# A two-layer attention and expert network on one core: three score banks in rotation, head pairs in halves of the partitions, a finer order of steps, and weights issued by GpSimd

## What is computed

```
x = x + xattn0(layernorm(x), ctx, ctx)     # 16 heads of 8, 512 keys, biases
x = x + ffn0(layernorm(x))                 # 8 experts 128-512-128, gelu, top 1 by a softmax gate
x = x + xattn1(layernorm(x), ctx)          # 16 query heads, 8 key heads, int8/ternary rounded
                                           # projections, a layernorm before the output projection
x = x + ffn1(layernorm(x))                 # shared expert + 15 experts 128-128-128, relu, top 3
scores = q @ k.T / sqrt(8); attn = softmax(scores); out = attn @ v      # per head
```

## Time and profile before

| | us |
|---|---|
| runs shown: 285.79, 287.11, 289.53; median | 287.11 |
| profiled execution, span from first to last instruction | 281.9 |
| median less span (start and end that the profile does not hold) | 5.2 |
| PE busy in the span | 235.6 |
| DVE busy | 177.7 |
| ACT busy | 145.3 |
| GpSimd busy | 54.4 |

### The profile page before, as it was taken

How to read it: one execution, slowest core, us unless ns; L and a number is a source line. 1 busy time by engine, 2 the same in 40 slices (tenths; PEclk the granted TensorE clock), 3 DMA queues, 4 the chain that set the end, 5 groups by cost and what they waited for, 6 DMA issues and landing times.

```text
span 281.9 us, 4880 instructions
## 1 busy us (share of the span) xinstructions
PE 235.6 (84%) x1685; PEld 152.1 (54%) x1700; DVE 177.7 (63%) x478; ACT 145.3 (52%) x336; POOL 54.4 (19%) x92
## 2 busy tenths in 40 slices
PE   2186345889999999999999999699699979889995
PEld 1035101344453545789988998343244424679985
DVE  5964797767656831421247137999577892589855
ACT  2026000657767686644435544366577678544542
POOL 8733982040402210100011300110000011021000
PEclk9999999799999999999999999959999999999999
DMA  6016327302270575800000110002100000000000
GB/s 158 0 60 226 150 72 162 110 4 80 74 205 22 149 190 137 215 5 2 1 0 0 58 56 2 1 0 58 56 4 0 3 0 0 3 0 0 21 1 20
DMA packets 20917, 16.26 MB, mean 58 GB/s; under 512 B 2085, under 2 KB 18989, under 8 KB 20797
## 3 DMA queue, kind: packets, MB, share of 16 engines
q1 hardware_dynamic: 20284, 15.76, 19.8%
q10 hardware_dynamic: 576, 0.13, 0.2%
q0 software_dynamic: 32, 0.07, 0.2%
HBM read 11.73 MB, written 4.19 MB: 56 GB/s over the span
## 4 chain that ended last, share of the span: by engine, by line
PE 65%; DVE 15%; ACT 7%; DMA 6%; issue 3%; SPq 2%; POOL 0%; DVEq 0%; ACTq 0%; another core or an unknown queue 0%
PE SB L1289 10%; PE OB L1226 8%; PE SA L1186 8%; DVE mx L906 7%; PE SB L1211 6%; PE OB L1302 5%; PE SB L1332 5%; PE SA L1302 5%; DMA Q<-nm 4%; PE SA L1342 4%; ACT prob L721 3%; DVE hn L871 3%; PE X L1154 2%; DVE qp L450 2%; PE X L1163 1%
## 5 line engine op out<-in xcount | busy, mean ns | idle before, releaser
L906 DVE TENSOR_REDUCE mx<-SA 128x1 bf16<-128x512 f32 x128 | 81.5, 686 | 20.0 <-PE SA L1186 15.9
L721 ACT ACTIVATE prob<-SB 128x512 f32<-128x512 f32 x128 | 69.4, 594 | 34.3 <-PE SB L1211 33.9
L1186 PE MATMUL SA<-K,Q 128*128 128x512 bf16 x113 | 41.5, 430 | 15.9 <-DVE mx L906 7.7
L1211 PE MATMUL SB<-Q,K 128*128 128x256 bf16 x256 | 41.6, 284 | 4.0 <-DMA Q<-nm 3.6
L782 ACT ACTIVATE prob<-SB,b1T 128x256 f32<-128x256 f32 x64 | 26.7, 471 | 28.5 <-PE SB L1289 28.4
L1226 PE MATMUL OB<-prob,V 128*32 128x256 f32 x512 | 39.7, 390 | 0.4 <-ACT oT L729 0.4
L1211 PEld LDWEIGHTS SB<-Q,K 128*128 128x128 bf16 x256 | 24.0, 101 | 24.9 <-ACT prob L721 6.8
L1289 PE MATMUL SB<-hT,w1s 128*128 128x256 f32 x128 | 33.3, 384 | 0.1
L1186 PEld LDWEIGHTS SA<-K,Q 128*128 128x128 bf16 x128 | 9.9, 102 | 35.6 <-DVE mx L906 23.9
L604 POOL TENSOR_SCALAR vareps<-mv 128x2 f32<-128x2 f32 x10 | 1.9, 192 | 137.2 <-DVE mv L850 137.2
L1289 PEld LDWEIGHTS SB<-hT,w1s 128*128 128x128 f32 x128 | 22.3, 190 | 3.6 <-ACT prob L782 0.7
(11 more groups left out here) (210 smaller groups left out, 282.4 us busy)
## 6 DMA issues: line engine op xcount, KB each, us to landing
w1s<-in_L_ffn_w_dram SPq DMA_DIRECT2D x8, 256.0 KB, 3.7
w2s<-in_L_ffn_w_dram SPq DMA_DIRECT2D x8, 256.0 KB, 4.4
K<-in_L_ffn_eW_dram SPq DMA_DIRECT2D x2, 960.0 KB, 6.5
K<-k_dram SPq DMA_DIRECT2D x8, 192.0 KB
Q<-q_dram SPq DMA_DIRECT2D x8, 192.0 KB
k_dram<-kp SPq DMA_DIRECT2D x2, 384.0 KB, 2.8
q_dram<-qp SPq DMA_DIRECT2D x4, 192.0 KB, 2.1
K<-k_dram SPq DMA_DIRECT2D x2, 384.0 KB
```

Source lines behind the costliest of these rows:

```text
L721: act.activation(prob[:, g % 2, i, 2 * u:2 * u + 2, :].rearrange("p k q -> p (k q)"), SB[u][:, :], ACT.Exp).then_inc(s_exp, 1)
L906: dve.tensor_reduce(mx[:, g % 2, r, i:i + 1], SA[SCORE_BANK[n]][:, :], AX, ALU.max).then_inc(s_sa_max, 1)
L1186: pe.matmul(SA[SCORE_BANK[u]][:, :], Q[n][:, b, s, r * P:(r + 1) * P], K[n][:, b, key_group(n, s), :], start=True, stop=True).then_inc(s_s ...
L1211: last = pe.matmul(SB[u][:, k * NQ:(k + 1) * NQ], K[n][:, b, key_group(n, s), kt * P:(kt + 1) * P], Q[n][:, b, s, :], start=True, stop=True)
```

## The change

One large rewrite of the order and of the layout of the stacks. In its parts:

- **Stack.** Row `8 * e + j` of the partitions now holds product `j` (0 to 5) of element `e`; `j` = 6 is the row of the maximum, `j` = 7 is zero. Head `2p` has partitions 0 to 63, head `2p + 1` has 64 to 127, so `Q` is half as large, and each score matmul reads 64 partitions (`rows`), the two heads of a pair alternating.
- **Write and read.** Each part is signalled, written once (one DMA each) as soon as it is made, and read back by six DMAs of 16 partitions each. ACT makes the first part straight from PSUM, DVE the rest. The queries of batch 0, layer 0 are read by ACT's queue.
- **Banks.** `X1` is now `SB[2]`: three `SB` banks rotate in attention, `X0` alone serves the small steps between the first and the last `exp` of a layer. The prologue uses idle `SA`, `SB`, `OB` banks.
- **Order.** Every `scores`, `values` and `max_rows` stands at a hand-written place; the lists are all new. The second batch's projections and `ctx_quant` come after the first `scores`. `values` waits for half a group's exponentials. `out_turn` and `bias0` are split or moved.
- **Who does what.** DVE zeroes `K[0]`, `Q[0]` (four memsets, now ahead of the first norm), GpSimd `K[1]`, `Q[1]`, `V` (smaller, 9 columns per head in place of 32). Some `max_rows`, `turn`, `vproj` copies move between ACT and DVE. GpSimd issues all bulk weights and small loads (`load`), and the row of ones of `K`.
- **Two DMAs** in place of one per `max_rows` (one per half).

```diff
-K_PART = (0, 1, 2, 0, 1, 0)
-SHIFT_ROW = 8 * len(K_PART)
-K_PARTS = ((2, 1), (1, 1))
+K_PART = (0, 0, 0, 1, 1, 2)
+SHIFT_ROW = 6
+STACK = 64
+K_PARTS = ((1, 1), (1, 1))
...
 IN_ATTENTION0 = {
...
+    (-2, 1): [('scores', 0, 3), ('scores', 1, 0)],
+    (-2, 2): [('zeros', 1, 1), ('max_rows', 0), ('values_ones', 1)],
+    (-2, 3): [('ctx_quant',)],
+    (-1, 0): [('w1_quant',), ('scores', 1, 1), ('qproj', 0, 1), ('vproj', 0, 1)],
+    (-1, 2): [('scores', 1, 2), ('scores', 1, 3)],
+    (-1, 3): [('kproj', 0, 1), ('ctxq_turn', 1), ('load_small', 0), ('ctxq_turn', 0), ('kstack', 0, 1),
+        ('scores', 2, 0)],
+    (0, 0): [('scores', 2, 1), ('max_rows', 1)],
...
+    (5, 2): [('out_turn', 0, 0, 0), ('kstack', 1, 1), ('scores', 7, 3), ('values', 4, 2)],
...
+    (7, 1): [('values', 6, 1), ('load_expert', 2), ('load_expert', 3)],
...
-        X = [stack.enter_context(nc.psum_tensor(f"X{n}", [P, 512], F32)) for n in range(2)]
-        YB = [OB, SA[2]]
+        X = [stack.enter_context(nc.psum_tensor("X0", [P, 512], F32)), SB[2]]
+        V0_BANK = [SA[2], OB]
+        YB = [SA[2], OB]
...
+        def read_stack(engine, dst, row_parts, dram, written, slots, done):
+            for part in range(3):
+                engine.wait_ge(written[part], 16)
+                for row in (j for j, p in enumerate(row_parts) if p == part):
+                    engine.dma_start(dst[row:P:8, slots].rearrange("e s c -> e (s c)"),
+                                     dram[part, :, slots].rearrange("e s c -> e (s c)")).then_inc(done, 16)
...
+                elif kind in LOADS and step not in ON_SYNC:
+                    load(pool, step)
...
+                    for a in range(2):
...
+                        rows = slice(64 * a, 64 * a + STACK)
+                        pe.matmul(SA[SCORE_BANK[u]][:, :], Q[n][rows, b, p, r * P:(r + 1) * P], K[n][rows, b, key_group(n, p), :],
                                   start=True, stop=True).then_inc(s_sa_full, 1)
...
+                    for a in range(2):
+                        m = 8 * gg + 2 * i + a
+                        if m >= 3:
+                            pe.wait_ge(s_exp, m - 2)
+                        rows = slice(64 * a, 64 * a + STACK)
                         for k in range(2):
                             kt = 2 * u + k
-                            last = pe.matmul(SB[u][:, k * NQ:(k + 1) * NQ],
-                                             K[n][:, b, key_group(n, s), kt * P:(kt + 1) * P], Q[n][:, b, s, :],
+                            last = pe.matmul(SB[m % 3][:, k * NQ:(k + 1) * NQ],
+                                             K[n][rows, b, key_group(n, p), kt * P:(kt + 1) * P], Q[n][rows, b, p, :],
                                              start=True, stop=True)
...
+                    if kt % 2 == 0:
+                        pe.wait_ge(s_exp, 8 * gg + 2 * kt + 4)
```

More of the change, by code:

```diff
@@ L78 @@
[L78 to L87, removed]
-IN_ATTENTION0 = {
[L89 to L110, removed]
@@ L111 @@
 }
 IN_EXPERTS00 = {
[L113 to L118, removed]
+    (-1, 1): [('out_turn', 0, 1, 0), ('out_turn', 0, 1, 1)],
+    (1, 0): [('att_turn', 0, 1)],
+    (1, 1): [('out_proj', 0, 1), ('stats', 'f0', 1)],
+    (3, 1): [('bias0', 0), ('norm', 'f0', 1)],
+    (6, 1): [('turn', 'f0', 1)],
+    (7, 0): [('red0', 1)],
@@ L119 @@
+    (7, 1): [('end0', 0)],
 }
 IN_EXPERTS01 = {
-    (-1, 0): [("end0", 0), ("stats", "q1", 0)],
-    (-1, 1): [("kstack", 1, 1), ("norm", "q1", 0), ("logits0", 1)],
-    (0, 0): [("quant", "q1", 0)],
-    (1, 0): [("bias0", 1), ("turn", "q1", 0)],
-    (1, 1): [("qproj", 1, 0)],
-    (4, 1): [("scores", 8, 0)],
-    (5, 0): [("scores", 8, 1)],
-    (5, 1): [("scores", 8, 2), ("qstack", 1, 0)],
-    (6, 0): [("scores", 8, 3)],
-    (6, 1): [("scores", 9, 0)],
+    (-1, 1): [('stats', 'q1', 0), ('logits0', 1)],
@@ L131 @@
+    (0, 1): [('norm', 'q1', 0)],
+    (1, 0): [('quant', 'q1', 0)],
+    (2, 0): [('turn', 'q1', 0)],
+    (2, 1): [('qproj', 1, 0)],
+    (5, 0): [('scores', 8, 0)],
+    (5, 1): [('scores', 8, 1), ('qstack', 1, 0)],
+    (6, 0): [('scores', 8, 2)],
+    (6, 1): [('scores', 8, 3)],
+    (7, 0): [('scores', 9, 0), ('scores', 9, 1)],
 }
 IN_ATTENTION1 = {
[L133 to L137 removed]
@@ L573, in _ @@
+                    for a in range(2):
+                        row = 64 * a + SHIFT_ROW
+                        sp.dma_start(Q[n][row:row + 1, b, 2 * g:2 * g + 2, :],
+                                     nm[2 * a:2 * a + 2, step[1] % 2, :]).then_inc(s_shift[step[1] % 2], 16)
+                elif kind in LOADS and step in ON_SYNC:
+                    load(sp, step)
                 elif kind == "store":
@@ L688, in _ @@
+                    parts_free(act, step)
+                    rows = P // (n + 1)
+                    dst, src = kp[0:rows, part_buffer(step), 0, :], xbank(step)[0:rows, :]
+                    if n == 0:
+                        act.wait_ge(in_bias0, 32)
+                        last = act.activation(dst, src, ACT.Identity, bias=bias3[:, 1:2])
+                    else:
+                        last = act.activation(dst, src, ACT.Copy)
+                    last.then_inc(s_kp[n][b], 1)
                 elif kind == "qproj":
@@ new lines, in _ @@
+                    u = part_buffer(step)
+                    if kind == "kproj":
+                        rows, bias, done = P // (n + 1), bias3[:, 1:2], s_kp[n][b]
+                        src, rest, parts = xbank(step)[0:rows, :], kr[0:rows, u, :], kp[0:rows, u, :, :]
+                    else:
+                        bias, done = bqs[:, :], s_qp[n][b]
+                        src, rest, parts = xbank(step)[:, 0:NQ], qr[:, u, :], qp[:, u, :, :]
+                    dve.wait_ge(done, 1)
+                    if n == 0:
+                        last = dve.scalar_tensor_tensor(rest, src, bias, parts[:, 0, :], ALU.add, ALU.subtract)
+                    else:
+                        last = dve.tensor_tensor(rest, src, parts[:, 0, :], ALU.subtract)
```

1017 lines of the change are left out of this document (598 added, 419 removed).

## The result

The changed kernel takes 275.66 us (median of 4 runs, 274.73 to 277.78), the kernel before 286.45 in the same session: a ratio of 0.9675, 95% interval 0.9587 to 0.9763. I forecast 262.5 us (248 to 277): the time lies inside the range, but the gain is 3.3% where I forecast 8.6%.

The account below looks back on a forecast made before the run. PE was taken to bound all but prologue and gap, DVE close behind in attention 1. Terms -5.8, -10, -1.3, 0, -6, -1.5 = -24.6 gave 257.3 us span, plus 5.2 to the median: 262.5 us, range 248 to 277.

Parts of the forecast that it names:

- The step: One attention step on PE: 1.55 us falls to 1.23 us, freeing 10 us of PE per layer.
- the bounds on the `scores` pair: Score matmuls in attention: nothing overlaps and a step keeps 1.55 us, or full overlap, `scores` part 0.33 instead of 0.54.
- Prologue: Start to first `exp`: first scores at 28 us against 34, first `exp` at 43.5 us against 49.3.
- +5.5: Prologue: DVE's four memsets, a reduce and the second stats stand before the norm, adding 5.5 us against 6.5 saved.
- Attention 0: First attention stage: 52 us against 62, from DVE's remaining scores steps, ACT's last `exp` steps, values and group 1's start.
- Experts and gap: Experts 0 65.4 us (-1), gap unchanged at 4 us, experts 1 37.4 us (-1.5).
- GpSimd's issues: Rival at the first `hidden0`: weight loads issued late while DVE and GpSimd hold each other up, 322 us; chance 0.03.
- Attention 1: Second attention stage: 55 us against 61, including +2 for batch 1's later queries.
- in part the slow clock at its start costs as now: Start of attention 1: the slow clock costs the same as before, 0.57 in 182 to 190 us.
- My 53: Attention 1 before the +2 for queries: 30.5 us and 9 us of DVE, 12.5 of `exp` steps, values 1.
- my marks of a wrong forecast: Steps of 1.5 us, stack waits over 2 us in attention, `hidden0` waiting for weights, or clock under 1 through much of attentions.
- PE stays the bound: Rival in both attentions: row halves do not overlap or switches eat the gain; 276.5 us, chance 0.20.

Follow-up runs that it names:

- the clearing run on all rows: Changed kernel with 128-row score matmuls, batch 0's layer-1 queries read for batch 1, SyncE's stack reads moved behind maxima rows, routed weights held for query reads: 276.80 us.
- the pair of cleared runs: Changed kernel without batch 1's layer-1 query wait, SyncE's stack reads moved, routed weights held: 276.80 us with 128-row score matmuls, 273.65 us in halves.

## Why the prediction was right and wrong

*The step.* Right. I took 1.23 us; it is 1.20. Of the bounds on the `scores` pair, overlap and no overlap, the lower came true, 0.30. By the Trainium skill, "TensorE: Matmul & The Clock Gate", Part 3, matmuls in different row groups run together, and the trace agrees; the drain at a change of tiling of its page "TensorEngine Tiling (Array Packing)", Key Properties, costs nothing beyond the 0.11 us that I had read from the trace. What I got wrong is who then bounds: where attention 0 runs steadily the chain still names PE at 1.20 a step and not DVE's reduces at 1.3, I take it because not every step has its two reduces. Over the whole of attention 0 PE is less than half of the chain; SyncE's stack reads (L510, 13%) and DMA landings stand beside it, and I had neither in the sum.

*Prologue.* 45.2 for 43.5. First reduce 29.9 us (28 forecast), `csq` from 36.99 to 42.94 (35.6 to 41.3), PE waiting for it with `exp 0` behind it, as described. The 1.7 us are within what the stack's landing with weights in flight costs: without them the first `exp` comes at 42.2. Of the memsets that I priced into +5.5, the 2.67 us that one run moved away are hidden.

*Attention 0.* 51.8 for 52, but partly by luck: other profiles of the same stage have 54.0 to 54.6. The mechanism holds in part: PE's busy time is 12.3 us less than before (58.43 to 46.09), but without the overlap the stage is 56.7 to 59.2 us, so the overlap gave 4 to 5 of the 10 us that I took for it, and the new order the rest.

*Experts and gap.* 67.1 for 65.4 and 39.5 for 37.4. The gains of 1 and 1.5 us that I gave to earlier norms and to halves among the experts did not come; PE is busy 65.29 us there, as before.

*GpSimd's issues.* Right. PE never waits for `w1s`, and no stall of several microseconds per issue shows.

*Attention 1.* Wrong: 64.8 for 55. Two terms of the sum failed. The step "from their projection to their use stand four `scores` steps, 5 us, and the way over DRAM takes some 8; +2" was mis-sized: the clearing run on all rows puts the whole of that way at 65.5 - 60.3 = 5.2 us, since the six reads also hold a row of maxima on SyncE and the routed weights are in flight beside the writes (2.9 us by itself, by the run in halves with all loads on SyncE). The larger one: "in part the slow clock at its start costs as now". It costs more. In halves PE's busy time fell from the 53.5 us before only to 52.5, though the work is less: 52.5 x 0.82 = 43.1 us at full clock, which is the 43 of my forecast. So the overlap was there, and the clock took 9.4 us of PE's time, against 53.5 x 0.06 = 3.2 before (estimates, since the clock is a mean over idle time too). With the way cleared it is 49.3 x 0.86 = 42.4 against 52.1 x 0.97 = 50.5 on all rows: 8 us less work, 2.8 us less busy time, 0.5 us less stage. How much the stage itself lost by the clock is shown only in that pair, 2.1 us ahead of the 17th exponential. The rest is no clock: behind it, at 1.00 in both, 5.1 us less of PE gave 2.5 us, since PE waits longer for others (in halves 3.9 us for maxima, 2.5 for exponentials, 1.8 for rows; 3.7, 1.8 and 0.8 on all rows). My 53 had the stage go by DVE's and ACT's work alone. The last of my marks of a wrong forecast, a clock under 1 through much of an attention, is what came; I had it as a mark and in no rival, so no time was worked out from it. Another, a wait of over 2 us for a stack inside an attention, came too, with 2.1 us.

*The rivals.* The time is within 1 us of the 276.5 that I gave to "PE stays the bound", and that is chance: its reason, halves that do not overlap or lose it all in switches, did not come, and its stages (60 and 61 us) are not those measured (51.8 and 64.8). My range holds the measured time only because I had drawn its upper end out to that rival.

By terms: prologue +1.7, attention 0 -0.2, experts 0 and gap +2.2, attention 1 +9.8 (about 3 the queries' way; the other 6.6 are the clock, of which PE's busy time allows at most some 6 and the pair of runs shows 2.1, and waits of PE that I had not counted, in shares that stay open), experts 1 +2.1: 15.6 of span. The median lay 2.8 us over the profiled span and not 5.2: -2.4, and 262.5 + 15.6 - 2.4 = 275.7.

What stays open: why the clock is low where it is. Shown is that of two orders alike in all but rows, the one on 64 rows without overlap stood at 0.70 and 0.58 and the one on 128 rows at 1.00 and 0.92, and that halves which overlap had 0.99 and 0.82. Whether it is the rows at work or the shorter busy stretches that overlap leaves in attention 1 isn't separated. A layout in halves that also keeps the clock up was not found, and no version beat the changed kernel by more than the measurement tells.

## What to carry to other kernels

An engine-time saving on PE is worth its size only at the clock that is granted afterwards: multiply PE's busy time by the granted clock of the stage, before and after, and if the product fell and the busy time did not, look for the clock and not for a new wait. And cut the stage where the clock changes: in the pair of cleared runs half of PE's saving reached the stage at full clock, and none where the clock was low. Before a chain of dependent transfers is moved into a busy stage, list what stands behind it on its queue and what is in flight beside it: here three delays covered each other in part. Taking out one gave 0 to 2.9 us, and all three together 5.

## What was not expected of the hardware

- With matmuls on 64 rows one after another the granted clock was low though PE was busy almost without a break: 0.70 and 0.58 at 97% busy, against 1.00 and 0.92 at 94% and 83% on 128 rows, 43 us on top of 281. The Trainium skill, "TensorE: Matmul & The Clock Gate", Part 1, has the gate follow how busy PE is; by the busy share alone the two runs should stand the other way round, and the measurement decides.
- At the lower level all three forms of the step take about twice as long, the overlapped ones too: 0.33, 0.30, 0.57 us against 0.56, 0.61, 1.01.
- With GpSimd's weight loads in flight the last read of the first key stack takes 6.38 us on the chain; with them held back, 4.53, though DMA was busy to only 0.40 over the prologue. In attention 1 the writes of the last stack of queries took 4.22 us to the first read with the routed weights issued ahead of them, and 1.68 with these issued behind.
